# One table with an order of its own for each engine, from the last attention head to the MLP's second piece

## The chip, the cores and the metric

The kernel runs on one core of a Trainium2 chip. The metric is the time of one execution on the device in microseconds. Before the change it is 1332.62 us, the median of three runs (1331.37 to 1333.58). TensorE, VectorE (DVE), ScalarE (ACT), GpSimd (POOL) and SyncE (SP) each run a program of their own, in order, and wait for each other by semaphores.

## What is computed

Two layers over x of 2 x 1024 x 512 (batch, tokens, width), each followed by a layer norm of x plus the layer's result. Layer 1 is attention with 16 heads of 128 in which a token sees its own block of 64 and two on either side. Layer 2 picks the 128 tokens of each batch with the highest router score, and runs causal attention over the 256 of them (16 query heads, 8 key and value heads, rotary positions) and a gated MLP of 2048; all other tokens pass.

```
x = layernorm(x + (softmax(q k^T * scale + band) v) @ Wo)      # q, k, v = x @ Wq, Wk, Wv
idx = sort(top_k(x @ w_router, 128)); s = x[idx]; h = rms_norm(s) * ln1_w
q, k, v = rope(h @ wq + bq), rope(h @ wk + bk), h @ wv + bv
x1 = s + (softmax(causal(q k^T / sqrt(128))) v) @ wo
p = x1 + (silu(h2 @ w_gate) * (h2 @ w_up)) @ w_down             # h2 = rms_norm(x1) * ln2_w
x = layernorm(x + x.at[idx].set(g * p + (1 - g) * s))           # g = sigmoid(router score)
```

## The kernel before

A planner in Python writes the list `order`: one entry per job, such as ("scores", 31, 4). `job` (L327) appends an entry and numbers the semaphore steps that the engines will make for it (`SIGNALS`). `hold` notes who had a buffer last, so that `freed` can tell whom the next user waits for. Then each of five programs (tensor L916, scalar, vector, gpsimd, sync) walks through the same list and does its own part of each job, if it has one. So all engines take the jobs in one common order.

The planner runs over u, a tile of 128 queries of a head: at each u it puts down the scores of tile u, the transposes of tile u-1, the weighing of values of u-3, a half of a projection of the next head, an output projection tile, and whatever running generators (`tick`, `FLOW`) offer. The jobs of the stretch in question are these:

- Layer 1, head 31, the last: `scores` (TensorE into bank s0 or s1; DVE mask and maximum L1414; ACT exponential L1218), `norm` (DVE reciprocal and product, L1423), `tp` (TensorE transposes L989; ACT first half and DVE second half of a split into two fp32r numbers, L1180, L1379), `pv` (TensorE), `ot` (ACT and DVE split of a piece of the head's output), `out` (TensorE output projection of a token tile into bank y; DVE adds it, L1466). `qkfirst` and `qk` are the two halves of a projection.
- End of layer 1 for a token tile: `ln` (DVE statistics L1480, POOL reciprocal root L1663 on), `lnorm` (ACT; SP stores the tile), `lnscore` (DVE product with the router's weights, L1490).
- Choosing tokens: `rows` (TensorE, L1040, and ACT put the scores along a row), `count` and `tie` (DVE comparisons, L1506, L1511), `rank`, `prefixmm`, `prefix`, `findmm`, `find` (to the index of each chosen token), `gather` (POOL, two indirect DMAs, L1718 and L1723), `rin` and `rinx` (DVE, ACT, POOL: gate and norm), `rinh` (TensorE transposes L1071, ACT copy).
- Layer 2 attention of batch b: `p2half` and `p2` (TensorE, the two halves of piece n of the q, k, v projections, and the bias matmul L1088, which needs `ubias`), `p2r` (DVE, rotation, L1577 to L1582), `p2t` (TensorE transposes into bank y, L1097, ACT copy L1184), `p2v` (ACT copy), then for each of 8 key heads `as2` (scores; DVE maximum L1595, ACT exponential L1317), `an2` (DVE reciprocal L1604, ACT product L1328), `at2` (TensorE L1119, ACT), `av2` (TensorE, ACT), `o2` (TensorE). After them `res` and `resh`.
- MLP: `gu` (gate and up of 128 columns), `down`. `wsplit.n.G` or `.V` is the split of a 512 KB weight piece: ACT first half, POOL (L1690, 2.4 us) or DVE second half. `wload` is its DMA.
- `hload.n` (SP, L1811): the 512 KB DMA of the nth piece of layer 2's attention weights into one of 8 places (homes). SP waits for the job that read the place last (`emptied_by`), and only then issues, in the order of the list: hload.8 to .11 wait for p2half.0.0, p2.0.0, p2half.0.1, p2.0.1, hload.19 (weights of o2.0.3) for o2.0.0, hload.24 (first half of p2.1.0) for o2.0.2, hload.43 (of o2.1.3) for o2.1.0.

In names, the number after the kind is the head or the batch, then comes the tile or piece: tp.31.4, p2.0.7, as2.1.3.

Of the kernel before, what the change touches and what calls it, by code (L numbers as in the profile page):

```python
# [152 lines left out]
def build(nc, x, Wq, Wk, Wv, Wo, w_router, wq, wk, wv, wo, w_gate, w_up, w_down, ln1_w, ln2_w, bqkv, rope, out):  # L153
    with ExitStack() as ctx:
# [603 lines left out]
        for u in range(END + 4):  # L758
            H, i = divmod(u, TT)
            r, G = u % (HG * TT), u // (HG * TT)  # L760
# [117 lines left out]
        def weights(*key):  # L880

# [38 lines left out]
        def tensor_program(e):  # L920
            pe = Lane(e)
            pe.wait_ge(*G_.at("const", "ident"))
            for kind, *key in order:
                if kind == "turn":
                    b, t = key
                    dst = bank[bank_of["turn", b, t]]
# [30 lines left out]
                elif kind == "v":  # L957
                    G, t = key
# [11 lines left out]
                elif kind == "scores":  # L970
                    H, i = key
                    js = key_tiles(i)
                    n = len(js) * P
# [18 lines left out]
                elif kind == "pv":  # L992
# [22 lines left out]
                elif kind == "out":  # L1015
                    G, t = key
# [57 lines left out]
                elif kind in ("p2half", "p2"):  # L1074
                    b, n = key
# [16 lines left out]
                elif kind == "p2t":  # L1092
                    b, n = key
# [6 lines left out]
                elif kind == "as2":  # L1100
                    b, n = key
# [10 lines left out]
                elif kind == "at2":  # L1112
                    b, n = key
# [61 lines left out]
        def scalar_program(e):  # L1175
# [7 lines left out]

                e.activation(dst, src, ACT.Copy).then_inc(*S_.inc(*name, "copy"))  # L1184

            for kind, *key in order:
                if kind == "turn":
                    b, t = key
                    if b > 0:
# [17 lines left out]
                elif kind == "v":  # L1207
                    G, t = key
# [5 lines left out]
                elif kind == "scores":  # L1214
                    H, i = key
                    s, n = i % 2, len(key_tiles(i)) * P
# [5 lines left out]
                elif kind == "tp":  # L1222
                    H, i = key
                    js = key_tiles(i)
                    n = len(js)
# [26 lines left out]
                elif kind == "wsplit":  # L1252
                    n, _ = key
# [41 lines left out]
                elif kind == "p2v":  # L1295
                    b, n = key
# [5 lines left out]
                elif kind == "p2t":  # L1302
                    b, n = key
# [7 lines left out]
                elif kind == "as2":  # L1311
                    b, n = key
# [8 lines left out]
                elif kind == "an2":  # L1321
                    b, n = key
# [8 lines left out]
                elif kind == "at2":  # L1331
                    b, n = key
# [35 lines left out]
        def vector_program(e):  # L1368
# [17 lines left out]
            e.memset(counts[:], 0.0)  # L1386
            after(e.memset(ones_bf[:], 1.0), "const", "small")

            for kind, *key in order:
                if kind == "turn":  # L1390
                    b, t = key
                    cols = slice(t * P, (t + 1) * P)
# [9 lines left out]
                elif kind == "v":  # L1402
                    G, t = key
                    lo_part(vv[1][:, t, :], bank["proj1"][:, 0:GW], vv[0][:, t, :], "v", G, t)

                elif kind == "scores":
                    H, i = key
                    s, n = i % 2, len(key_tiles(i)) * P
# [8 lines left out]
                elif kind == "norm":  # L1417
                    H, i = key
                    s, n = i % 2, len(key_tiles(i)) * P
# [6 lines left out]
                elif kind == "tp":  # L1426
                    H, i = key
                    js = key_tiles(i)
                    n = len(js)
# [28 lines left out]
                elif kind == "out":  # L1458
                    G, t = key
# [9 lines left out]
                elif kind == "wsplit" and key[1] == "V":  # L1469
                    n = key[0]  # L1470
# [384 lines left out]
```

## Time and profile before

| | before |
|---|---|
| median of three runs | 1332.62 us |
| the profiled execution | 1332.4 us |
| its span, first to last instruction | 1330.3 us |
| TensorE busy | 1279.7 us (96%) |
| DVE, ACT, POOL busy | 781.6, 602.9, 243.3 us |
| mean granted TensorE clock | 0.986 |

The span starts at 0 with the first instruction. Head 31 begins at about 1048.5 us, layer 2's first projection at 1084.6, batch 1's first projection at 1170 and the MLP at 1251. The profiled execution takes 2.1 us more than its span. Busy time of TensorE can hold time in which its clock is lower: the granted clock stands beside it. "A <- B" in the views means that an instruction of A started late because of B.

### The profile page before, as it was taken

Reading aid. Unit: us, or ns where it says so; the run is one execution under the profiler, and the core shown is the slowest. Engines: PE = TensorE matmul, PEld = TensorE weight load, DVE = VectorE, ACT = ScalarE, POOL = GpSimd, SP = SyncE. Lnnn points to the kernel's source line nnn. Section 1 sums busy time; section 2 is a strip of 40 time slices with the busy share of each in tenths; the row PEclk is TensorE's granted clock in tenths of the full one; section 3 lists DMA queues with packets and bytes.
Section 4 is the critical chain, followed back from the end, with each engine's and each line's share of the span. In section 5 each row is a group of like instructions: output and inputs, shape, how many; then the busy total and the mean of one; then the engine's idle time right before and its main releaser. Section 6 shows DMA issues by size and latency. Waiting matters only on the chain.

```text
span 1330.3 us, 18968 instructions
## 1 busy us (share of the span) xinstructions
PE 1279.7 (96%) x7296; PEld 1092.9 (82%) x7296; DVE 781.6 (59%) x2187; ACT 602.9 (45%) x1422; POOL 243.3 (18%) x218
## 2 busy tenths in 40 slices
PE   7999999999999999999999999999999978999897
PEld 6898989898989898978798989898989853545696
DVE  4656565656665656676667765656565667542243
ACT  4544445454444444545444444444444442433453
POOL 2101111111111110134120212111111142000064
PEclk9999999999999999999999999999999988999899
DMA  5000111110001202032310101010101055565064
GB/s 183 31 33 32 33 32 32 33 32 33 33 32 33 80 1 79 1 103 90 109 49 17 48 28 46 28 48 17 48 17 48 27 180 162 184 208 162 0 198 135
DMA packets 62410, 89.33 MB, mean 67 GB/s; under 512 B 3232, under 2 KB 36000, under 8 KB 62320
## 3 DMA queue, kind: packets, MB, share of 16 engines
q1 hardware_dynamic: 61904, 86.81, 20.0%
q0 software_dynamic: 416, 1.31, 0.3%
q8 instruction: 57, 0.93, 0.3%
q14 instruction: 33, 0.27, 0.1%
HBM read 79.20 MB, written 8.91 MB: 66 GB/s over the span
## 4 chain that ended last, share of the span: by engine, by line
PE 87%; DVE 7%; ACT 4%; issue 1%; POOL 1%; DMA 1%; SPq 0%; POOLq 0%
PE proj L909 41%; PE y L909 13%; PE s L909 10%; PE o L909 9%; PE tp L989 5%; PE proj L917 3%; PE s L917 3%; DVE arena L1379 2%; ACT arena L1180 2%; PE o L917 1%; ACT prob L1218 1%; DVE prob L1414 1%; DVE products L1490 1%; DVE prob L1423 1%; DVE yacc L1466 1%
## 5 line engine op out<-in xcount | busy, mean ns | idle before, releaser
L909 PE MATMUL proj<-arena 128*128 128x256 f32 (+1 forms) x3408 | 625.5, 332 | 7.2 <-DVE arena L1379 6.3
L909 PEld LDWEIGHTS proj<-arena 128*128 128x128 f32 x3408 | 521.8, 190 | 65.4 <-DVE arena L1379 8.2
L1218 ACT ACTIVATE prob<-prob,stat 128x384 f32<-128x384 f32 (+1 forms) x256 | 151.0, 590 | 443.5 <-DVE stat L1414 443.5
L1690 POOL TENSOR_TENSOR arena<-wraw,arena 128x1024 fp32r<-128x1024 f32 x75 | 182.2, 2439 | 832.3 <-ACT arena L1180 814.0
L1379 DVE TENSOR_TENSOR arena<-proj,arena 128x512 fp32r<-128x512 f32 (+1 forms) x256 | 142.7, 558 | 274.2 <-ACT arena L1180 272.4
L909 PE MATMUL y<-arena 128*128 128x512 f32 x810 | 211.0, 396 | 0.3 <-DVE yacc L1466 0.3
L1379 DVE TENSOR_TENSOR arena<-tp,arena 128x384 fp32r<-128x384 f32 (+2 forms) x258 | 134.9, 523 | 108.4 <-ACT arena L1180 108.2
L909 PE MATMUL o<-arena 128*128 128x256 f32 (+2 forms) x960 | 196.2, 324 | 0.5 <-DVE arena L1379 0.5
L909 PE MATMUL s<-arena 128*128 128x384 f32 (+2 forms) x870 | 191.5, 333 | 3.0 <-DVE arena L1379 3.0
L1180 ACT ACTIVATE arena<-proj 128x512 fp32r<-128x512 f32 (+1 forms) x256 | 124.3, 486 | 118.5 <-PE proj L909 115.5
L909 PEld LDWEIGHTS s<-arena 128*128 128x128 f32 x870 | 151.8, 189 | 20.3 <-DVE arena L1379 4.5
L909 PEld LDWEIGHTS y<-arena 128*128 128x128 f32 x810 | 147.4, 189 | 24.7 <-DVE yacc L1466 0.7
L909 PEld LDWEIGHTS o<-arena 128*128 128x128 f32 x960 | 136.8, 190 | 1.7 <-DVE arena L1379 1.2
L1414 DVE CUSTOM_DVE_ANT_0 prob<-s,band 128x384 f32<-128x384 f32 (+1 forms) x256 | 131.9, 515 | 0.0
L989 PE MATMUL tp<-ident,prob 128*128 128x128 f32 x704 | 119.9, 274 | 7.1 <-DVE prob L1423 7.1
L1180 ACT ACTIVATE arena<-tp 128x384 fp32r<-128x384 f32 (+2 forms) x258 | 117.9, 457 | 10.5 <-PE tp L989 7.9
L1423 DVE TENSOR_SCALAR prob<-prob,stat 128x384 f32<-128x384 f32 (+1 forms) x256 | 113.8, 445 | 9.1
L989 PEld LDWEIGHTS tp<-ident,prob 128*128 128x128 f32 x704 | 85.9, 140 | 24.7 <-DVE prob L1423 13.9
L1466 DVE TENSOR_TENSOR yacc<-y,yacc 128x512 f32<-128x512 f32 x127 | 87.1, 686 | 17.1 <-PE y L909 17.0
L1180 ACT ACTIVATE arena<-wraw 128x1024 fp32r<-128x1024 f32 x88 | 90.3, 1055 | 2.3 <-DMA wraw<-in_L_ffn_w_up 1.8
L917 PE MATMUL proj<-late 128*128 128x512 f32 x120 | 58.6, 612 | 0.0
L1180 ACT ACTIVATE arena<-o 128x512 fp32r<-128x512 f32 (+1 forms) x74 | 42.0, 568 | 22.6 <-PE o L1071 14.7
(156 smaller groups left out, 686.0 us busy)
## 6 DMA issues: line engine op xcount, KB each, us to landing
wraw<-in_L_attn_Wq SPq DMA_DIRECT2D x16, 512.0 KB, 3.4
wraw<-in_L_attn_Wk SPq DMA_DIRECT2D x16, 512.0 KB, 3.3
wraw<-in_L_attn_Wv SPq DMA_DIRECT2D x16, 512.0 KB, 3.4
wraw<-in_L_attn_Wo SPq DMA_DIRECT2D x16, 512.0 KB, 3.7
late<-in_L_ffn_wq SPq DMA_DIRECT2D x16, 512.0 KB, 4.7
late<-in_L_ffn_wo SPq DMA_DIRECT2D x16, 512.0 KB, 3.9
yacc<-in_L_attn_hidden_states SPq DMA_DIRECT2D x16, 256.0 KB, 3.0
y_dram<-yacc SPq DMA_DIRECT2D x16, 256.0 KB, 3.0
```

The lines of the kernel that those rows point to most:

```text
L909: ins = e.matmul(out_ap, l[a], r[b], start=first and i == 0 and j == 0, stop=final and i == n - 1 and j == 2, skip_group_check=skip)
L917: ins = e.matmul(out_ap, l, r, start=first and i == 0, stop=final and i == n - 1, skip_group_check=skip)
L989: ins = e.transpose(bank["tp"][:, m * P:(m + 1) * P], prob[i % 2][:, m * P:(m + 1) * P], ident[:])
L1180: e.activation(dst, src, ACT.Copy).then_inc(*S_.inc(*name, "hi"))
L1218: e.activation(prob[s][:, 0:n], prob[s][:, 0:n], ACT.Exp, bias=stat[:, 4 * s + 1:4 * s + 2], scale=-1.0, accum_out=stat[:, 4 * s + 2:4 * s ...
L1379: e.tensor_tensor(dst_lo, src, dst_hi.bitcast(F32), ALU.subtract).then_inc(*V_.inc(*name, "lo"))
L1414: e.tensor_tensor_reduce(prob[s][:, 0:n], bank[f"s{s}"][:, 0:n], reach, -SCALE, -NEG, ALU.add, ALU.min, nm).then_inc(*V_.inc("scores", H, ...
L1423: e.tensor_scalar(prob[s][:, 0:n], prob[s][:, 0:n], rc, None, ALU.mult).then_inc(*V_.inc("norm", H, i, "prob"))
L1466: e.tensor_tensor(yacc[:, t, :], bank[bank_of["out", G, t]][:, :], yacc[:, t, :], ALU.add).then_inc(*V_.inc("out", G, t, "sum"))
L1490: e.tensor_tensor_reduce(products[:], row, router[:], 1.0, 0.0, ALU.mult, ALU.add, score[:, c:c + 1]).then_inc(*V_.inc("lnscore", b, t, "s ...
L1690: e.tensor_tensor(lo, wraw[n % RAW_SLOTS][:], hi.bitcast(F32), ALU.subtract).then_inc(*G_.inc("wsplit", n, "lo"))
```

## The change

`job` no longer numbers steps; it only notes what the job holds. A new function `comes(n, engines)` gives job n to some engines: it appends it to their programs, numbers their steps, and settles at the first call who frees the buffers. All jobs before scores.31.0 are given to all engines, in the old order. Then the table `LAST` is read: each word is an engine (T, S, V, G) and a job. Whatever it doesn't name comes afterwards in the old order. No word of the table names D, the program of SP, so SP's list is the old one. It names 164 jobs of TensorE, 158 of DVE, 134 of ACT and 19 of POOL, from scores.31.0 to gu.1 and the weight splits behind it. The instructions of a job are not touched.

The buffers' succession stays the same but for bank y: p2t.0.0 now has it between out.15.5 and out.15.6, and before it came after out.15.6.

How far jobs move in an engine's list, the larger moves:

- TensorE: scores.31.1 to 31.7 come 3 to 6 jobs earlier, rinh.0 7 later; p2t.0.0 4 earlier, out.15.6 and 15.7 3 later; p2.0.4 to p2.0.7 2 to 11 earlier, with av2.0.0 9 later, o2.0.0 11, o2.0.1 10, o2.0.2 8, o2.0.3 9; rinh.1 4 later, after o2.0.6. In batch 1 p2.1.4 to p2.1.7 are 1 to 9 earlier, o2.1.0 15 later, o2.1.1 14.
- DVE: rin.0 13 and rinx.0 11 earlier, ubias 18 later, p2r.0.0 13 earlier, p2r.0.4, p2r.0.5 11 earlier; ln.1.7 12 later, lnscore.1.7 14 later, the split of weight piece 68 19 later.
- ACT: rinh.0 7 later, lnorm.1.7 4 later, splits 66 and 67 19 and 47 later, split 68 19 earlier.
- POOL: split 65 behind ln.1.2, 66 behind ln.1.3, 67 behind gather.1.

```diff
+LAST_HEAD = ("scores", 31, 0)
+LAST = """
+S.scores.31.0 S.tp.30.7 S.rin.0 S.qk.31.k.1 S.scores.31.1 S.tp.31.0 S.scores.31.2 S.o.30.1 S.tp.31.1 S.scores.31.3
+S.qk.31.q.1 S.tp.31.2 S.tp.31.3 S.scores.31.4 T.scores.31.0 T.qkfirst.31.k.1 T.scores.31.1 T.tp.30.7 T.qk.31.k.1
+T.scores.31.2 T.out.14.4 T.tp.31.0 T.pv.30.5 T.pv.30.6 T.scores.31.3 T.out.14.5 T.pv.30.7 T.tp.31.1 T.qkfirst.31.q.1
+T.qk.31.q.1 T.tp.31.2 T.out.14.6 T.scores.31.4 T.tp.31.3 T.scores.31.5 T.pv.31.0 T.out.14.7 T.pv.31.1 T.tp.31.4
+T.scores.31.6 T.pv.31.2 T.out.15.0 T.tp.31.5 T.scores.31.7 T.rinh.0 T.pv.31.3 T.out.15.1 T.pv.31.4 T.tp.31.6
...
+V.out.15.2 V.ln.1.2 V.lnscore.1.0 V.ot.4 V.tp.31.7 V.out.15.3 V.lnscore.1.1 V.ubias V.ot.5 V.lnscore.1.2 V.ln.1.3
+V.count.1.0.0 V.out.15.4 V.count.1.1.before V.p2r.0.0 V.ot.6 S.wsplit.65.G S.scores.31.5 S.ot.0 S.tp.31.4 S.ot.1
...
+S.tp.31.7 S.ot.5 S.lnorm.1.2 S.rows.1.0 S.ot.6 G.rin.0 G.ln.1.0 G.ln.1.1 T.out.15.2 T.p2half.0.0 T.tp.31.7 T.pv.31.5
+T.out.15.3 T.pv.31.6 T.p2.0.0 T.rows.1.0 T.out.15.4 T.pv.31.7 T.p2half.0.1 T.out.15.5 T.p2.0.1 T.p2t.0.0
+T.p2half.0.2 T.rows.1.1 T.out.15.6 T.out.15.7 T.p2t.0.1 T.p2.0.2 T.p2half.0.3 S.lnorm.1.3 S.wsplit.66.G S.p2t.0.0
...
+T.as2.0.0 T.p2.0.3 T.as2.0.1 T.rows.1.2 T.p2half.0.4 T.p2.0.4 T.p2half.0.5 T.p2t.0.3 T.p2.0.5 T.at2.0.0 T.as2.0.2
+T.p2half.0.6 T.at2.0.1 T.p2t.0.4 T.rows.1.3 T.p2.0.6 T.as2.0.3 T.av2.0.0 T.p2half.0.7 T.p2t.0.5 T.p2.0.7 T.at2.0.2
+T.as2.0.4 T.av2.0.1 T.o2.0.0 T.at2.0.3 T.as2.0.5 T.av2.0.2 T.o2.0.1 T.av2.0.3 T.p2t.0.7 T.prefixmm.1 T.at2.0.4
+T.o2.0.2 T.findmm.1 T.as2.0.6 T.av2.0.4 T.at2.0.5 T.o2.0.3 T.as2.0.7 T.at2.0.6 T.av2.0.5 T.o2.0.4 T.av2.0.6
+T.at2.0.7 T.o2.0.5 T.av2.0.7 T.o2.0.6 T.rinh.1 T.o2.0.7 T.p2half.1.0 T.p2.1.0 T.p2half.1.1 T.p2.1.1 V.count.1.4.3
...
+G.ln.1.2 G.wsplit.65.G G.ln.1.3 G.wsplit.66.G G.ln.1.4 G.ln.1.5 G.ln.1.6 G.ln.1.7 G.gather.1 G.wsplit.67.G G.rin.1
...
+"""
...
         def job(kind, *key):
             order.append((kind,) + key)
-            if kind == "wsplit":
...
+            taken.append(taking[:])
+            taking.clear()
...
+        program = {eng: [] for eng in "TVSGD"}
+
+        def comes(n, engines):
+
+            kind, *key = order[n]
+            for space, who, steps, name in taken[n]:
+                room[who, space] = holder.get(space)
+                holder[space] = (steps, name)
+            taken[n] = []
+            signals = SIGNALS["wsplit" + key[1] if kind == "wsplit" else kind] if kind in SIGNALS or kind == "wsplit" else {}
+            for eng in engines:
+                program[eng].append(order[n])
+                for name in signals.get(eng, ()):
+                    ENGINES[eng].plan(kind, *(key[:1] if kind == "wsplit" else key), name)
...
+        turning = number_of[LAST_HEAD]
+        for n in range(turning):
+            comes(n, "TVSGD")
+        placed = set()
+        for line in LAST.split():
+            eng, kind, *key = line.split(".")
+            n = number_of[(kind,) + tuple(int(k) if k.isdigit() else k for k in key)]
+            comes(n, eng)
+            placed.add((eng, n))
+        for n in range(turning, len(order)):
+            comes(n, [eng for eng in "TVSGD" if (eng, n) not in placed])
...
-            for kind, *key in order:
+            for kind, *key in program["T"]:
```

The other four programs read `program["S"]`, `["V"]`, `["G"]` and `["D"]` likewise.

## Rows read from the trace of the kernel before

**Rows 1.** The page: span, and TensorE and its granted clock in 40 slices

```profile
span 1330.3 us, 18968 instructions
...
PE   7999999999999999999999999999999978999897
...
PEclk9999999999999999999999999999999988999899
```

**Rows 2.** Windows: from:to length, busy us (instructions) PE PEld DVE ACT POOL, clock, DMA

```profile
1048.50:1060.80 12.30, 12.30 (x65) 10.53 (x64) 7.61 (x21) 4.19 (x11) 0.00 (x0) 1.00 0.01 2
1060.80:1104.00 43.20, 35.90 (x149) 25.14 (x148) 30.06 (x85) 17.12 (x38) 21.03 (x41) 0.92 0.53 178
1104.00:1122.50 18.50, 13.68 (x32) 5.90 (x30) 12.59 (x46) 4.84 (x12) 5.00 (x12) 0.72 0.44 148
1122.50:1157.70 35.20, 31.67 (x122) 16.32 (x122) 22.29 (x96) 12.96 (x45) 0.00 (x0) 1.00 0.62 194
1157.70:1170.00 12.30, 11.45 (x42) 7.42 (x42) 4.59 (x19) 7.73 (x24) 2.80 (x4) 0.87 0.43 148
1170.00:1246.00 76.00, 70.26 (x233) 37.48 (x232) 23.45 (x73) 28.36 (x74) 0.74 (x2) 1.00 0.45 145
1246.00:1252.00 6.00, 1.46 (x8) 1.25 (x9) 3.54 (x7) 1.88 (x2) 0.74 (x2) 0.80 0.00 0
```

**Rows 3.** Windows, same columns: the stretches with a lower granted clock

```profile
1068.00:1076.00 8.00, 6.60 (x24) 5.25 (x23) 4.95 (x15) 5.27 (x12) 3.78 (x2) 0.57 0.88 331
...
1109.00:1120.00 11.00, 9.31 (x17) 4.09 (x17) 6.25 (x25) 2.49 (x4) 2.16 (x5) 0.53 0.25 85
...
1156.00:1162.00 6.00, 4.51 (x15) 3.48 (x16) 2.11 (x10) 3.25 (x11) 2.05 (x2) 0.72 0.42 137
```

**Rows 4.** Timeline of TensorE: start, us, instruction, [idle before <-who ended it]

```profile
1067.30 0.55 PE L989 MATMUL tp<-ident,prob 128*128 128x128 f32 x3 [1.91 <-DVE prob L1423]
...
1108.45 0.63 PE L1097 MATMUL y<-ident,late 128*128 128x128 f32 x4 [3.14 <-DVE late L1582]
...
1157.49 1.12 PE L1097 MATMUL y<-ident,late 128*128 128x128 f32 x4 [1.93 <-DVE late L1582]
```

**Rows 5.** Waits of TensorE, 1048 to 1252: us in total, times, longest

```profile
PE y L1097 <- DVE late L1582: 8.9, 6, 3.1
PE tp L989 <- DVE prob L1423: 4.8, 4, 1.9
...
PE o L1040 <- DVE score L1490: 1.6, 1, 1.6
```

**Rows 6.** Timelines of DVE and of POOL, in the last head

```profile
1074.76 2.38 DVE L1423 TENSOR_SCALAR prob<-prob,stat 128x384 f32<-128x384 f32 x1
...
1072.22 4.70 POOL L1690 TENSOR_TENSOR arena<-wraw,arena 128x1024 fp32r<-128x1024 f32 x2 [6.19 <-ACT arena L1180]
```

**Rows 7.** The page's costliest groups: line, engine, shapes | busy us, mean ns

```profile
L1218 ACT ACTIVATE prob<-prob,stat 128x384 f32<-128x384 f32 (+1 forms) x256 | 151.0, 590 | 443.5 <-DVE stat L1414 443.5
...
L1414 DVE CUSTOM_DVE_ANT_0 prob<-s,band 128x384 f32<-128x384 f32 (+1 forms) x256 | 131.9, 515 | 0.0
...
L1423 DVE TENSOR_SCALAR prob<-prob,stat 128x384 f32<-128x384 f32 (+1 forms) x256 | 113.8, 445 | 9.1
```

**Rows 8.** The router products' line: duration ns min/median/max, first and last start

```profile
L1490 DVE CUSTOM_DVE_ANT_0 products<-yacc,router x16: 680/683/2344, 576.4 to 1112.6; 128x512 bf16<-128x512 f32 x16
```

**Rows 9.** DMA issues, 1110 to 1222: KB each, median us to landing

```profile
late<-in_L_ffn_wq SPq DMA_DIRECT2D x10, 512.0 KB, 4.5
```

**Rows 10.** The chain that ended last: start, us, what

```profile
1159.32 2.96 DMA late<-rope,position
...
1170.19 1.72 PE proj L917 x4
1171.91 1.72 PE s L917 x4
```

**Rows 11.** Waits of DVE, 1048 to 1252: us in total, times, longest

```profile
DVE arena L1379 <- ACT arena L1180: 15.6, 12, 2.4
...
DVE stat L1604 <- ACT prob L1317: 6.9, 6, 1.2
DVE yacc L1466 <- PE y L909: 6.2, 5, 4.0
```

More of the change, by code:

```diff
@@ new lines @@
+T.p2half.0.2 T.rows.1.1 T.out.15.6 T.out.15.7 T.p2t.0.1 T.p2.0.2 T.p2half.0.3 S.lnorm.1.3 S.wsplit.66.G S.p2t.0.0
+S.rows.1.1 S.lnorm.1.4 V.lnscore.1.3 V.out.15.5 V.ln.1.4 V.count.1.1.0 V.tie.1.0 V.ln.1.5 V.p2r.0.1 V.out.15.6
+V.tie.1.1 V.ln.1.6 V.count.1.0.1 V.out.15.7 V.count.1.1.1 V.lnscore.1.4 V.lnscore.1.5 V.lnscore.1.6
+V.count.1.2.before V.count.1.2.1 V.as2.0.0 V.count.1.3.before V.count.1.3.1 V.tie.1.2 V.ln.1.7 V.p2r.0.3 V.as2.0.1
+V.tie.1.3 V.an2.0.0 V.count.1.0.2 V.count.1.1.2 V.p2r.0.4 V.count.1.2.2 V.lnscore.1.7 V.count.1.3.2 V.an2.0.1
@@ new lines @@
+V.count.1.4.before V.p2r.0.5 V.as2.0.2 V.count.1.4.2 V.count.1.5.before V.count.1.5.2 V.tie.1.4 V.tie.1.5
+V.count.1.0.3 V.an2.0.2 V.as2.0.3 V.count.1.1.3 V.count.1.2.3 V.count.1.3.3 S.p2t.0.1 S.lnorm.1.5 S.lnorm.1.6
+S.as2.0.0 S.rows.1.2 S.p2v.0.2 S.lnorm.1.7 S.an2.0.0 S.p2t.0.3 S.as2.0.1 S.at2.0.0 S.an2.0.1 S.as2.0.2 S.p2t.0.4
+S.rows.1.3 S.as2.0.3 S.at2.0.1 S.an2.0.2 S.av2.0.0 S.p2t.0.5 S.an2.0.3 S.at2.0.2 S.av2.0.1 S.as2.0.4 S.at2.0.3
+S.wsplit.67.G S.av2.0.2 S.wsplit.68.V S.an2.0.4 S.p2v.0.6 S.as2.0.5 S.at2.0.4 S.p2t.0.7 S.av2.0.3 S.an2.0.5
@@ new lines @@
+V.count.1.5.3 V.an2.0.3 V.count.1.6.before V.count.1.6.3 V.count.1.7.before V.as2.0.4 V.p2r.0.7 V.count.1.7.3
+V.an2.0.4 V.tie.1.6 V.tie.1.7 V.rank.1 V.as2.0.5 V.prefix.1 V.an2.0.5 V.find.1 V.as2.0.6 V.an2.0.6 V.as2.0.7
+V.an2.0.7 V.rin.1 V.rinx.1 S.av2.0.4 S.as2.0.6 S.at2.0.5 S.an2.0.6 S.at2.0.6 S.as2.0.7 S.av2.0.5 S.an2.0.7 S.av2.0.6
+S.at2.0.7 S.av2.0.7 S.rinh.1 S.rin.1 S.resh.0 S.p2t.1.0 S.p2v.1.2 S.p2t.1.1 S.p2t.1.3 S.as2.1.0 S.an2.1.0 S.as2.1.1
+S.at2.1.0 S.as2.1.2 S.an2.1.1 S.at2.1.1 S.an2.1.2 S.as2.1.3 S.p2t.1.4 S.an2.1.3 S.av2.1.0 S.p2t.1.5 S.at2.1.2
@@ new lines @@
+G.ln.1.2 G.wsplit.65.G G.ln.1.3 G.wsplit.66.G G.ln.1.4 G.ln.1.5 G.ln.1.6 G.ln.1.7 G.gather.1 G.wsplit.67.G G.rin.1
+G.res.0 G.res.1 T.p2t.1.0 T.p2half.1.2 T.p2.1.2 T.p2half.1.3 T.resh.0 T.p2.1.3 T.p2t.1.1 S.av2.1.1 S.at2.1.3
+S.as2.1.4 S.av2.1.2 S.p2t.1.7 S.an2.1.4 S.as2.1.5 S.av2.1.3 S.an2.1.5 S.at2.1.4 S.as2.1.6 S.p2v.1.6 S.at2.1.5
+S.an2.1.6 S.av2.1.4 S.as2.1.7 S.av2.1.5 S.at2.1.6 S.an2.1.7 V.p2r.1.0 V.p2r.1.1 V.res.0 V.resh.0 V.p2r.1.3 V.as2.1.0
+V.an2.1.0 V.as2.1.1 V.an2.1.1 V.p2r.1.4 V.as2.1.2 V.p2r.1.5 V.as2.1.3 V.an2.1.2 V.an2.1.3 V.p2r.1.7 V.as2.1.4
@@ L127, in compares @@
+T.gu.1 G.gu.0 G.gu.1 G.wsplit.70.G S.resh.1 V.res.1 V.resh.1 V.gu.0 V.gu.1 V.wsplit.69.V S.gu.0 S.gu.1 S.wsplit.69.V
+S.wsplit.70.G
+"""
 def compares():
@@ L329, in build @@
         ENGINES = dict(T=T_, V=V_, S=S_, G=G_)
-        order = []
+        order, taken, taking = [], [], []
         holder, room = {}, {}
@@ L1184, in whole_copy @@
                 e.activation(dst, src, ACT.Copy).then_inc(*S_.inc(*name, "copy"))
-            for kind, *key in order:
+            for kind, *key in program["S"]:
                 if kind == "turn":
@@ L1387, in vector_program @@
             after(e.memset(ones_bf[:], 1.0), "const", "small")
-            for kind, *key in order:
+            for kind, *key in program["V"]:
                 if kind == "turn":
@@ L1683, in gpsimd_program @@
             pool.wait_ge(*V_.at("const", "small"))
-            for kind, *key in order:
+            for kind, *key in program["G"]:
                 if kind == "wsplit" and key[1] == "G":
@@ L1758, in sync_program @@
             sp = Lane(e)
-            for kind, *key in order:
+            for kind, *key in program["D"]:
                 if kind == "router":
```

21 lines of the change are left out of this document (12 added, 9 removed).

## The prediction

> **What bounds the kernel now.** I first read the page's 40 slices [rows 1]. The reader should see TensorE at nine tenths nearly everywhere and its granted clock below full in the last fifth. The span is 1330.3 us. Next I cut the changed stretch into windows [rows 2]: from 1048.5 us, where the last head's scores begin, to 1246, where batch 1's output projection ends. TensorE idles 5.7 + 1.6 us in the last head and the end of layer 1 (7.3 in the window 1060.8 to 1104, 5.7 of it before 1084.6), 18.50 - 13.68 = 4.8 at the layer change, 3.5 during batch 0's attention, 0.85 to 1170 and 5.7 in batch 1. That is 22.2 us. Another 4.5 us lie behind 1246.
>
> The granted clock is a second loss [rows 3]. While it was 0.57, 6.60 us were busy, which is 6.60 x 0.43 = 2.8 us lost. The other two are 9.31 x 0.47 = 4.4 and 4.51 x 0.28 = 1.3, together 8.5. A piece of idle time lies in front of each, or at its start: 1.91 us ending at 1067.30, 3.14 ending at 1108.45 and 1.93 ending at 1157.49 [rows 4]. The first two windows are nearly all at the lower level (1.2 GHz), the third for about half its time, and from 1122.5 to 1157.7 the grant is 1.00 (2.4 GHz) [rows 2, 3]. So 22.2 + 8.5 = 30.7 us is all that an order can give here: the matmuls stay the same.
>
> Third, the waits [rows 5]. 8.9 us of them are a transpose of a rotated q or k that waits for DVE's sum, 4.8 are probability transposes waiting for DVE's normalisation, and 1.6 the scores' rows waiting for a router product. All are waits for one job of an engine that is itself not full: DVE is busy 7.6 + 30.1 + 12.6 + 22.3 = 72.6 of the 109.2 us up to the index of the chosen tokens [rows 2]. TensorE's own work up to there is 12.3 + 35.9 + 13.7 + 31.7 = 93.6 less 7.2 of clock, that is 86.4. TensorE is therefore the bound if both are fed, with DVE second.
>
> **The change, part by part.** No instruction is added or dropped; the jobs' numbers follow each engine's new list. SP ("D") is in no line of the table and keeps the old order.
>
> *Last head.* TensorE now issues scores.31.1 and scores.31.2 ahead of transposes 30.7 and 31.0, so that a tile's chain (mask and maximum, exponential, normalisation, transpose, two splits) runs a tile ahead. The 1.91 us [rows 4] are such a transpose waiting. Stepping through the new list with the durations of the timelines, each transpose's probabilities are there 0.4 to 1.7 us before TensorE comes to it, and the splits of the last head's output (ot) 0.1 to 1.3 us. The idle 5.7 and the 2.8 of clock go, and I leave 1.0: +7.5 (bounds 8.5 and 1.7, if three waits of the size of 1.91 and half the clock remain). DVE's routing work of batch 0 (rin.0, rinx.0) comes earlier in it, beside out.14 jobs that keep TensorE busy.
>
> *POOL.* The weight splits 65 and 66 move behind ln.1.2 and ln.1.3, and 67 behind the gather. Now splits 66 and 67 hold POOL for 4.70 us, and DVE's normalisation beside them takes 2.38 us [rows 6] where its mean is 0.45 [rows 7]. One blocked DVE instruction costs 1.93, and that one goes (it is in the 7.5). In their new place the splits run beside router products, the bias split (ubias) and a rope sum. The router product has been blocked too: 2.344 us against a median of 0.683 [rows 8]. ubias stands right in front of the bias matmul of p2.0.0. I put one block of 1.7 on TensorE's path there, and 0.8 for pv.31.6, which follows transpose 31.7 with less between than before. The rows.1.0 wait of 1.6 [rows 5] goes, as it now comes after p2.0.0 and pv.31.6. This piece is 1.6 - 2.5 = -0.9; its bounds are +1.6 (no block) and 1.6 - 5.1 - 0.8 = -4.3 (three blocks).
>
> The page SBUF — State Buffer of the Trainium skill, section Who interferes with whom, states this as a rule: a DVE instruction with two SBUF inputs, or one in a 2-port mode, and a GpSimd instruction that reads SBUF exclude each other for a whole instruction. The two long rows agree. By that rule alone, any of the splits that meets such a DVE instruction would add up to 2.4 us to DVE; without it this part would be a gain of 1.6.
>
> *Layer change.* p2t.0.0 moves ahead of out.15.6 and out.15.7, p2r.0.0 ahead of ot.6 and the ties on DVE. Before, DVE came to p2r.0.0 only behind lnscore.1.4, ln.1.6 and ln.1.7, and TensorE waited 3.14 us for it [rows 4]. Now ln.1.7 comes 12 places later. Of 4.8 idle and 4.4 clock I leave 1.0: +8.2 (bounds 9.2 and 3, with two waits of 1 to 2 us and the clock low again). What is late next is lnscore.1.7, 14 places later: rows.1.3 needs it, and it is some 2.6 us ahead of TensorE in my stepping. On SP the store of that tile (lnorm.1.7) stands before hload.13, and behind it queue loads 14 to 18. I have it issued some 8 us before p2.0.6 needs it; a load lands in 4.5 us [rows 9], so 3 us are to spare.
>
> *Batch 0.* TensorE does all projections (p2.0.3 to p2.0.7) first and puts off av2 and o2: o2.0.0 by 11 places. This fills the wait for the softmax with 1.72 us pieces [rows 10] and brings p2r.0.7 out of the token chain's way. New waits: all as2.0.x share bank s0, and as2.0.5 waits for DVE's maximum of as2.0.4, behind two long counts (about 0.9); prefixmm waits for rank (0.9). Behind findmm stand 4 attention quarters with four o2 of 1.72, about 10.2 us, over the chain find, gather (its second DMA 2.96 [rows 10]), rin, rstd, rinx of about 8.7: 1.5 to spare, and I allow 1.5 of idle, since DVE may still be at an2.0.7. Loss before: 3.5 + 0.85 + 1.3 = 5.7. I leave 3.5 (0.9, 0.9, 1.5 and 0.2): +2.2. Bounds: +5.7 and -6.
>
> *SP's unchanged order.* hload.19 waits for o2.0.0, and loads 20 to 23, needed by o2.0.4 to o2.0.7, stand behind it; 24 and 25 (batch 1's first piece) wait for o2.0.2. From o2.0.0 to o2.0.3, which reads load 19, TensorE has 7.3 us of other work against the 4.5 of a load. Batch 1 is alike: load 43 opens at o2.1.0, and 7.8 us lie before o2.1.3. I cost it at nothing; the cover is 2.8 us, and if gone a load costs up to 4.5. wload.68 has to wait for split 65, which ends around 1083 in the new order, before hload.11: nothing.
>
> *Batch 1.* The same shift (o2.1.0 by 15 places) takes the rope waits out: 5.7, of which I leave 1.5: +4.2 (bounds 5.7 and 1.5). The end (res.1, resh.1, 4.5 us idle [rows 2] and the clock of 0.80 there) has the same chain and stays.
>
> Sum: 7.5 - 0.9 + 8.2 + 2.2 + 4.2 = 21.2. Span 1330.3 - 21.2 = 1309.1. The profiled execution took 1332.4, 2.1 more than its span: 1311.2. The median of the runs, 1332.62, is 0.2 above it: **1311.5 us**. Differences of under about 0.2% (2.7 us) cannot be told from no change here.
>
> **Rivals.**
> (a) *DVE becomes the bound.* For: it has waited 15.6 us for ScalarE's first halves and 6.2 for TensorE's out [rows 11], and an in-order engine keeps such waits if the neighbours shift with it. If they and the 6.9 for exponentials stay, DVE needs 72.6 + 28.7 = 101.3, plus 3.7 for blocks less 1.93, about 103 of the 109.2 us: 6 us gained there, 4.2 in batch 1, 1332.6 - 10.3 = 1322. Against: ot, tp and out now have a job of another kind between them nearly everywhere. 12%.
> (b) *Nearly everything closes.* All 30.7 would give 1302; with a fourth of my 9.5 left over, 1304. 10%.
> (c) *Slower: the weights.* Place: SP's queue, loads 19 to 33 and 43 to 47, now opened by postponed o2 jobs. If a load is opened only one piece before it is needed, a piece of 1.72 us [rows 10] hides less than half of its 4.5 us and TensorE waits 2.8 each time. Fifteen such waits are 42 us: 1332.6 - 21.2 + 42 = 1353. It decides for slower from 9 such waits on (23.9 / 2.8). Against: the 7.3 us counted above; none of the waits named above is for a landing. 5%.
> (d) *The order changes nothing*, since the two prob buffers set the pace and not the lists. Against: maximum 0.52, exponential 0.59, normalisation 0.45 [rows 7] and transposes 0.55 [rows 4] are 2.1 us for a buffer, one tile in 1.1 us with two, and between 1060.8 and 1104 TensorE has (35.9 - 2.8) / 5 = 6.6 us of work for each of the five tiles left [rows 2, 3]. Within 0.2%: 3%.
>
> **How the numbers follow.** Forecast 70% (own range 1304 to 1320, with the 9.5 of residues between a fourth and nearly twice), (a) 12%, (b) 10%, (c) 5%, (d) 3%. The range must leave out no more than 2 in 10: 1303.5 takes in half of (b), 1321 a part of (a). Faster: 70 + 12 + 10 = 92, less 1 for the part of (a) that runs out near nothing, 91%; same 3%; slower 6%.
>
> **What would show it.** Right: no idle over 1 us before the probability transposes of head 31; p2half.0.0 starting 8 to 9 us earlier than 1084.6; clock 1.00 through the layer change; DVE busy above 80% up to the index; batch 1's first piece near 1144 to 1150 instead of 1170; the distance from there to the MLP 4 us shorter. Wrong: a TensorE wait that a weight's DMA ends (c); findmm later than 1148 (a); a router product, ubias or rope sum of 2.3 us more than once; rinh.1 with idle of over 2 us before it.

## The result, and the profile after

The changed kernel takes 1300.29 us (median of 4 runs, 1299.84 to 1302.11) and the kernel before, run beside it, 1333.1 (ratio 0.9753, 95% interval 0.9731 to 0.9775). My forecast was 1311.5, with a range from 1303.5 to 1321. The direction was right, and the gain of 33 us is half as large again as the 21.2 I had summed, outside the range.

The page of the changed kernel (the profiled execution took 1302.1 us), in the same rows as [rows 1]: span, then busy time and the clock granted to TensorE in 40 slices.

```profile
span 1300.3 us, 18971 instructions
PE 1267.5 (97%) x7296; PEld 1089.4 (84%) x7296; DVE 783.2 (60%) x2187; ACT 600.4 (46%) x1422; POOL 243.8 (19%) x218
...
PE   7999999999999999999999999999999999999897
...
PEclk9999999999999999999999999999999999999899
```

The dent in TensorE's row and the two slices of its clock at eight tenths beside it are gone; the one at the MLP's start is left. The instructions are as before: the same work, in other turns.

Next the waits of TensorE from 1048 to 1222 us in the changed kernel (us in total, times, longest), which answer to [rows 5], and their places in its timeline (idle time in brackets), which answer to [rows 4]:

```profile
PE o L1145 <- DVE works L1695: 3.3, 1, 3.3
PE proj L1162 <- DVE arena L1529: 2.1, 1, 2.1
PE o L1145 <- DVE works L1632: 1.1, 1, 1.1
PE y L1171 <- DVE yacc L1540: 0.5, 1, 0.5
```

```profile
1076.24 1.88 PE L991 MATMUL proj<-late 128*128 128x512 f32 x4
...
1084.57 0.49 PE L1162 MATMUL proj<-arena,unit_row 40*128 40x512 f32 x1 [2.07 <-DVE arena L1529]
...
1094.44 0.66 PE L1171 MATMUL y<-ident,late 128*128 128x128 f32 x4 [0.46 <-DVE yacc L1540]
...
1147.42 0.66 PE L1145 MATMUL o<-ident,works 128*128 128x128 f32 x4 [1.15 <-DVE works L1632]
...
1219.57 1.09 PE L1145 MATMUL o<-ident,works 128*128 128x128 f32 x4 [3.31 <-DVE works L1695]
```

Twenty-six idle pieces of over 0.1 us have become five: those of the four rows with brackets, and 1.41 us right behind the last of them. No probability transpose waits any more, and no transpose of a rotated q or k waits for its rotation: from 1147.4 to 1216, all of batch 1, there is no idle time. The first row is layer 2's first projection, 8.3 us earlier than in the kernel before. Three waits are left ahead of the MLP. The bias matmul of p2.0.0 waits for `ubias`, which is two instructions of DVE, the unit row (L1525) and the lower half of the split behind it (L1529): 2.07. The transposes p2t.0.0 wait for bank y, which the residual sum of out.15.5 has to free: 0.46. And rinh.1 waits for the end of the token chain: 1.15.

In the windows the changed stretch, up to the MLP's first matmul, reads as follows, first in the kernel before and then in the one after (from:to, length, busy us and instructions of PE, PEld, DVE, ACT and POOL, granted clock, DMA's share, GB/s):

```profile
1048.75:1251.17 202.42, 175.63 (x639) 102.95 (x637) 103.09 (x342) 76.57 (x203) 30.31 (x61) 0.95 0.46 149
```

```profile
1050.30:1222.07 171.77, 163.38 (x637) 99.63 (x636) 105.24 (x342) 74.32 (x203) 31.71 (x61) 0.98 0.51 175
```

The stretch is 30.65 us shorter. Idle time gives 26.79 - 8.39 = 18.4 of it. The other 12.25 are *busy* time, for the same matmuls. The clock accounts for part: before, 8.5 were lost [rows 3]; after, there is one fall ahead of 1216, in the window of 8 us behind the 2.07 us wait, and it costs 7.43 x 0.21 = 1.6:

```profile
1084.00:1092.00 8.00, 7.43 (x23) 5.25 (x24) 6.49 (x17) 2.42 (x4) 3.31 (x7) 0.79 0.31 106
```

So 12.25 - 6.9 = 5.3 us of busy time are neither recorded idle time nor clock. My sum had no term for them.

### The profile page after: what moved, and what is told of

Same layout as the page of the kernel before. It is cut to its first block, busy times and chain, and to the rows that moved or that the text cites. A ratio compares the mean times of both kernels' runs of the same rounds, so it can differ in the third digit from the quotient of the medians.

```text
span 1300.3 us, 18971 instructions
## 1 busy us (share of the span) xinstructions
PE 1267.5 (97%) x7296; PEld 1089.4 (84%) x7296; DVE 783.2 (60%) x2187; ACT 600.4 (46%) x1422; POOL 243.8 (19%) x218
## 4 chain that ended last, share of the span: by engine, by line
PE 89%; DVE 5%; ACT 3%; DMA 1%; issue 1%; POOL 1%; SPq 0%; POOLq 0%; ACTq 0%
PE proj L983 42%; PE y L983 13%; PE s L983 10%; PE o L983 9%; PE tp L1063 5%; PE proj L991 4%; PE s L991 2%; DVE arena L1453 2%; ACT arena L1254 1%; PE o L991 1%; ACT prob L1292 1%; DVE products L1564 1%; DVE prob L1488 1%; DVE yacc L1540 1%; DMA wraw<-in_L_attn_Wq 0%
## 5 line engine op out<-in xcount | busy, mean ns | idle before, releaser
L1254 ACT ACTIVATE arena<-tp 128x384 fp32r<-128x384 f32 (+2 forms) x258 | 118.0, 457 | 12.9 <-PE tp L1063 10.3
```

The source lines that it names most:

```text
L1254: e.activation(dst, src, ACT.Copy).then_inc(*S_.inc(*name, "hi"))
```

## The experiments

Two theories on the missed 11 us were set against each other first. Theory H: every wait of TensorE costs some 0.2 us more than its recorded idle time. Theory P: the sum was right in kind, and the surplus lies in batch 1. Three kernels build the change up piece by piece, and a fourth run repeats the whole.

In the diffs below a line is a run of words of one engine's list around the edit, not a line of the file; the words that follow are left out at the marks.

**l1_head.** The table's new order ends with the last head (TensorE's words are shown); the jobs behind it have the old order. The weight splits are an exception here and in the next two kernels: they keep the table's new places on POOL and ScalarE.

```diff
 T.tp.31.7 T.pv.31.5 T.out.15.3
-T.pv.31.6 T.p2.0.0 T.rows.1.0 T.out.15.4 T.pv.31.7 T.p2half.0.1
+T.rows.1.0 T.p2.0.0 T.pv.31.6 T.out.15.4 T.p2half.0.1 T.pv.31.7
...
```

> The table's own orders only for the jobs up to tp.31.7 (the last head); every later job in the old common order. Nothing is left out of the computation. Theory H (every wait of TensorE hides some 0.2 us more than its recorded idle time, because the end of the matmul before it is modelled later than the next one could start): the head's recorded loss of 5.7 idle and 2.8 clock plus 8 waits x 0.2 go, 1333.1 - 9.5 = about 1323.5. Theory P (the prediction's sum was right in kind, the surplus is batch 1's): 1333.1 - 7.5 = 1325.5.

Measured 1322.34 us (1321.95 to 1325.57), against 1332.3 of the kernel before on the same chip: -10.0, where my term for the head was 7.5 (and a part of POOL's -0.9, which comes with the splits, is in it too). The early head meets a layer change in the old order, and a wait for a rope sum stands there that is larger than any of the kernel before. TensorE's timeline of this kernel:

```profile
1080.55 0.43 PE L1113 MATMUL o<-ident,score 128*128 128x128 f32 x2 [1.59 <-DVE score L1563]
...
1101.13 1.09 PE L1170 MATMUL y<-ident,late 128*128 128x128 f32 x4 [4.57 <-DVE late L1655]
1103.42 1.11 PE L1170 MATMUL y<-ident,late 128*128 128x128 f32 x4 [1.20 <-ACT late L1257]
```

**l2_change.** The new order ends at layer 2's fifth projection half (p2half.0.4).

```diff
 T.rows.1.2 T.p2half.0.4
-T.p2.0.4 T.p2half.0.5 T.p2t.0.3 T.p2.0.5
+T.at2.0.0 T.p2t.0.3 T.p2.0.4 T.av2.0.0
...
```

> The table's own orders up to p2half.0.4 (last head and layer change), the old common order from there on. Theory H: the head's 9.5, then 1.6 + 9.2 of recorded loss and 3 waits x 0.2, less the 2.1 us wait for ubias and the clock behind it (1.6): 1333.1 - 17.5 = about 1315.5. Theory P: 1333.1 - 14.8 = 1318. The trace shows in both the wait of the bias matmul L1162 of about 2.1 us.

Measured 1319.04 (1316.87 to 1320.75): -3.3 more, where the terms of POOL and of the layer change were 7.3 together. The 4.57 us are gone, but behind the new order batch 0's old one waits 1.9 us for a rope sum, 2.6 for probabilities and 2.5 for copies of ScalarE (L1257), and the bias matmul's wait is now 2.1 (0.78 in l1_head).

**l3_batch0.** The new order ends ahead of batch 1, which has the old one.

```diff
 T.rinh.1
-T.o2.0.7 T.p2half.1.0 T.p2.1.0
+T.p2half.1.0 T.o2.0.7 T.p2.1.0
...
```

> The table's own orders up to the end of batch 0 (before p2half.1.0), batch 1 in the old common order. Theory H: batch 1 keeps its recorded 5.4 to 5.7 us of idle time and 7 waits x 0.2, so this is 7.1 slower than the changed kernel: 1307.5. Theory P: the surplus of 11 us over the prediction lies in batch 1, so this is 4.2 + 11 = 15 slower than the changed kernel: 1315.

Measured 1311.44 (1310.7 to 1315.14): -7.6 more, where the term was 2.2.

**after_again.** The changed kernel without an edit, on the same chip.

> The changed kernel on the same chip as its three parts: 1300.3 in both theories, 0.9753 of the kernel before; it fixes the distance to the three others.

Measured 1300.79 (1300.34 to 1302.27): -10.65 more, where the term was 4.2. The increments 10.0, 3.3, 7.6 and 10.65 sum to 31.5 against 21.2. By these times neither theory holds throughout: measured were 1322.3, 1319.0 and 1311.4, where H had 1323.5, 1315.5 and 1307.5 and P had 1325.5, 1318 and 1315. Neither had an entry for the waits that a part moved alone hands on to the next.

More than half of the difference of 10.3 comes with batch 1, the simplest of the parts. From the start of its first projection piece to the start of its last output piece, less a piece of batch 0 of 1.72 us where one stands inside, the traces have 72.1 us before, 73.2 in l3_batch0 and 64.8 after. That is 7.4 to 8.4, where the recorded idle time that went is only 5.6 to 6.2, in 7 and 8 waits, and the granted clock is 1.00 in all three. So a part without any routing work and without a fall of the clock gives about 2 us more than its idle time. (The step of 10.65 is larger than 8.4 because l3_batch0's profile has the fall behind the 2.07 us wait, 1.7 us, and after_again's has not, and a wait of 0.69 stood in front of batch 1.)

To see what, I split the same stretch of every kernel, from the end of scores.31.0 to the end of the first gate/up piece: its length, TensorE's recorded idle time, the number of waits of over 0.1 us, busy time lost to a lower clock (busy time times one less the granted clock), and the rest.

| kernel | stretch | idle | waits | clock | rest |
|---|---|---|---|---|---|
| before | 207.8 | 26.8 | 26 | 11.8 | 169.2 |
| l1_head | 197.4 | 23.0 | 19 | 6.4 | 168.0 |
| l2_change | 194.5 | 20.6 | 18 | 6.2 | 167.8 |
| l3_batch0 | 185.8 | 15.4 | 14 | 3.9 | 166.4 |
| after | 176.2 | 8.4 | 5 | 3.8 | 164.0 |
| after_again | 174.7 | 8.3 | 5 | 2.2 | 164.2 |
| both (below) | 173.1 | 6.4 | 3 | 2.7 | 164.0 |
| both_outfirst (below) | 171.4 | 4.8 | 2 | 2.7 | 164.0 |

The rest is the same matmuls at full clock in all rows. It falls with the number of waits, from 26 to 5 by 5.0 to 5.2 us, 0.24 for each, and is 164.0 to 164.2 with five or fewer; the four profiles that the table leaves out (control, ubias_early, pool_late, sp_follows, 4 or 5 waits) have 163.7 to 164.1. The number of falls of the clock goes down as well, but it isn't the reason: "after" has one more than after_again and no larger rest.

The reason can be read from rows. Here are two output projection pieces of the kernel before, four matmuls each of one shape, the first behind a wait and the second in a full queue:

```profile
1167.81 1.95 PE L917 MATMUL s<-late 128*128 128x512 f32 x4 [0.40 <-ACT late L1184]
...
1171.75 1.88 PE L917 MATMUL s<-late 128*128 128x512 f32 x4
```

In the full queue the four are shown as 1.88 us, but the next matmul starts 1.71 us after their start. The end of a matmul is modelled, and where TensorE waits idle time is counted only from that modelled end, 0.16 us late. And the first matmul behind a wait takes longer: it is shown with 0.67 us instead of 0.59 (128x512), a transpose with 0.30 to 0.33 instead of 0.27. Over the 20 waits of the kernel before that lie outside the falls of the clock, the two together are 0.22 us on average, which is read from single instructions and not from the table. In the trace the weight load of such a matmul starts only 0.03 us ahead of it; that this makes it longer I only argue.

The next kernels ask what the waits that are left come from. Theory A: the job stands too late in its engine's list. Theory B: POOL's weight split holds up DVE. The rows that led to the question are these, of DVE and then of POOL in the changed kernel:

```profile
1081.51 2.29 DVE L1525 TENSOR_TENSOR unit_row<-ident 40x8 fp32r<-40x8 f32 x1
...
1091.25 2.52 DVE L1564 CUSTOM_DVE_ANT_0 products<-yacc,router 128x512 bf16<-128x512 f32 x1
```

```profile
1081.37 2.41 POOL L1764 TENSOR_TENSOR arena<-wraw,arena 128x1024 fp32r<-128x1024 f32 x1
...
1090.80 2.42 POOL L1764 TENSOR_TENSOR arena<-wraw,arena 128x1024 fp32r<-128x1024 f32 x1 [1.97 <-ACT arena L1254]
```

**ubias_early.** DVE's list alone is edited.

```diff
-V.ot.2 V.out.15.1
+V.ot.2 V.ubias V.out.15.1
...
-V.lnscore.1.1 V.ubias V.ot.5
+V.lnscore.1.1 V.ot.5
```

> The changed kernel with one word moved: DVE splits the bias rows (ubias) right behind ot.2, before POOL's weight split 65 can start. Theory B (POOL's split, which begins 0.14 us before, blocks DVE's two-input instruction and with it the bias matmul of p2.0.0): the wait of 2.07 us before L1162 goes, with 0.24 hidden behind it and in some executions 1.6 of clock; DVE is 0.9 later for the last head, which costs at most 0.5: 1300.5 - 2.3 to - 3.9, about 1297.5. Rival (the bias matmul would wait anyway, for p2.0.0's turn in DVE's or ScalarE's list): within 0.5 of the changed kernel.

Measured 1299.0 (1298.69 to 1300.03), 1.4 under the unchanged copy (control, below), where 2.3 to 3.9 under it were expected. The unit row takes 0.15 us, the 2.07 us wait is gone, and no clock fall follows. But the splits now hold up two router products (one in the changed kernel), and TensorE's wait in front of p2t.0.0 grows to 1.66. DVE's rows and TensorE's row of this kernel:

```profile
1081.73 2.54 DVE L1563 CUSTOM_DVE_ANT_0 products<-yacc,router 128x512 bf16<-128x512 f32 x1
...
1088.58 2.59 DVE L1563 CUSTOM_DVE_ANT_0 products<-yacc,router 128x512 bf16<-128x512 f32 x1
```

```profile
1091.84 0.66 PE L1170 MATMUL y<-ident,late 128*128 128x128 f32 x4 [1.66 <-DVE yacc L1539]
```

**pool_late.** DVE's list as in the changed kernel, POOL's edited.

```diff
-G.ln.1.2 G.wsplit.65.G G.ln.1.3 G.wsplit.66.G
+G.ln.1.2 G.ln.1.3 G.wsplit.65.G G.wsplit.66.G
```

> Only POOL's order differs from the changed kernel: its split of weight 65 stands behind its part of the LayerNorm of tile 3 of layer 1, instead of in front of it; VectorE's unit row stays where the change put it. Theory B (the small two-input instruction of VectorE is slow because POOL's 128x1024 subtraction reads at the same time): the row of unit_row is 0.15 us instead of 2.29, and TensorE's wait of 2.07 us before the bias matmul shrinks by about 2 us, to under 0.5; the split now meets another two-input instruction of VectorE, so time comes out 0 to 2 us under the changed kernel's 1300.4. Theory A (the job stands too late in VectorE's own turns, POOL has nothing to do with it): the row stays above 2 us or the wait stays near 2.07 us.

Measured 1303.08 (1299.17 to 1304.64): the time is 2.7 over the unchanged copy, where 0 to 2 under it were expected; the mechanism is as theory B has it. With ubias where the change put it, its instruction takes 0.15 us and the 2.07 us wait is gone. The two splits now run back to back, 5.14 us from 1087.36 on, and hold up two other instructions that read two operands from SBUF. DVE's rows:

```profile
1082.21 0.15 DVE L1524 TENSOR_TENSOR unit_row<-ident 40x8 fp32r<-40x8 f32 x1
...
1087.67 2.62 DVE L1655 TENSOR_TENSOR late<-late 128x512 f32<-128x512 f32 x1
...
1090.55 2.50 DVE L1563 CUSTOM_DVE_ANT_0 products<-yacc,router 128x512 bf16<-128x512 f32 x1
```

and TensorE's wait with the window behind it, where the granted clock is 0.50, the lower level (1.2 GHz), for 6.8 us:

```profile
1093.72 1.12 PE L1170 MATMUL y<-ident,late 128*128 128x128 f32 x4 [2.73 <-DVE yacc L1539]
```

```profile
1092.80:1099.60 6.80, 5.88 (x13) 3.52 (x14) 4.87 (x15) 1.49 (x3) 4.21 (x12) 0.50 0.00 0
```

One block of 2.1 us has become 1.9 + 1.8, and 5.88 x 0.50 = 2.9 us of clock came with it. The splits are as long as before; what they meet on DVE has changed. Not all of the 2.7 us is the edit's: this profile has another fall of 6.8 us from 10.7 us on, far ahead of the edit, with 6.07 us busy in it, 3.0 us lost.

**sp_follows.** Words for SP: loads that need not wait for o2.0.0 go ahead of load 19, which does, and the same in batch 1.

```diff
+D.hload.18 D.hload.20 D.hload.22 D.hload.23 D.hload.25 D.hload.27 D.hload.19 D.hload.21 D.hload.24
...
+D.hload.30 D.hload.32 D.hload.31 D.hload.33
...
+D.hload.42 D.hload.44 D.hload.46 D.hload.47 D.hload.43 D.hload.45
```

> The changed kernel with a list for SP too: the weight loads 19 to 30 and 39 to 47 in the order in which their places come free in TensorE's new list (20, 22, 23, 25, 27 ahead of 19, and so on), the rest as it was. Theory Q (SP's old order holds the free places back until o2.0.0 and then lets nine loads go at once, which stretches the rope gather from 3.0 to 6.4 us and makes rinh.1 wait 0.7 to 1.15): that wait goes, and the DMA share between 1114 and 1130 us rises from 0.06 to over 0.4: 1300.5 - 1.2 = 1299.3. Rival (the gather is late for its own reasons): the gather stays above 5 us and the time within 0.4 of the changed kernel.

Measured 1300.54 (1299.24 to 1301.22): no difference from the unchanged copy that can be told. The trace did change. In the changed kernel SP stood from 1113.5 at load 19 until o2.0.0 was made, and then issued nine loads of 512 KB within 9.4 us (1130.0 to 1139.4), beside the gather that the token chain waits for. Its chain there:

```profile
1136.56 1.10 POOL x_sel L1792
1137.66 0.30 issue
1137.96 6.35 DMA late<-rope,position
1144.31 0.02 issue
1144.33 0.69 DVE products L1621
```

The second gather took 6.35 us, where it took 2.96 before [rows 10]. The windows 1114 to 1130 and 1136 to 1145 show the burst, in the changed kernel and then in sp_follows:

```profile
1114.00:1130.00 16.00, 16.00 (x61) 8.48 (x60) 13.80 (x59) 8.56 (x31) 0.00 (x0) 1.00 0.42 155
...
1136.00:1145.00 9.00, 9.00 (x37) 5.54 (x37) 2.25 (x15) 5.57 (x20) 4.42 (x3) 1.00 0.98 357
```

```profile
1114.00:1130.00 16.00, 16.00 (x65) 8.90 (x64) 13.79 (x58) 8.36 (x32) 0.00 (x0) 1.00 0.87 309
...
1136.00:1145.00 9.00, 9.00 (x33) 5.14 (x32) 3.41 (x15) 5.32 (x19) 5.12 (x5) 1.00 0.74 226
```

With DMA at 0.74 instead of 0.98, the second gather takes 3.50 us, DVE has the gathered rows 5.4 us after the index, not 8.3, and TensorE's wait before rinh.1 (1.15) is gone from the trace. All profiles agree: 5.9 to 6.4 us for this gather in the five kernels with the whole table and SP's old order, 3.2 to 3.5 in the three with SP's new one. (The expectation's 0.06 is the DMA share of 1120 to 1130; from 1114 to 1130 it is 0.42.) Worth at most 1.15 + 0.24 us, it does not show in the medians.

**both.** The edits of ubias_early and sp_follows together.

> Both edits together, the moved ubias and SP's own list. If they are independent, 1300.5 - 2.9 - 1.2 = 1296.4, with idle time left only at the MLP's start (3.3 + 1.4) and 0.5 to 0.8 us before the first rope transpose. If the time saved ahead only brings TensorE sooner to a token chain that isn't ready, rinh.1 waits again and it is no better than the better of the two (1297.5).

Measured 1298.48 (1297.43 to 1299.03), 1.9 under the unchanged copy: short of the 1296.4, since the moved ubias alone had already brought 1.4 and not 2.9. rinh.1 doesn't wait, so the other case isn't what happened either. Ahead of the MLP only the wait of 1.66 is left.

**control.** The changed kernel, unchanged, beside these three.

> The changed kernel once more as the measure for the three others: 1300.5, 0.9755 of the kernel before, in both theories. Its profile shows whether the clock falls behind the 2.07 us wait (1302 in the profiled execution) or not (1300.3).

Measured 1300.37 (1299.86 to 1302.43). Its profiled execution, the one of 1302.43, has the fall behind the wait (2.06).

**both_outfirst.** In both, DVE does the residual sum that TensorE waits for, and one LayerNorm's moments, ahead of the router product that the split would hold up.

```diff
-V.lnscore.1.3 V.out.15.5 V.ln.1.4 V.count.1.1.0
+V.out.15.5 V.ln.1.4 V.lnscore.1.3 V.count.1.1.0
```

> The version with both edits (1298.5 us), and in it VectorE adds the last y piece of group 15's tile 5 and takes the moments of tile 4 ahead of the router product of tile 3, which POOL's split holds up for 2.6 us. If the 1.66 us wait of TensorE that is left in the layer change comes only from that place in the queue, it goes, and the time is 1.7 + 0.24 = 1.9 us lower, 1296.6 (1296.0 to 1297.5). If the split then holds up the next job just as long, the wait only moves on and the time stays at 1298.5 within 0.5.

Measured 1297.29 (1296.05 to 1297.67), ratio 0.9725 (0.9707 to 0.9743), against 0.9746 (0.9729 to 0.9763) of both: the fastest here, some 3 us under the changed kernel, and 0.7 above the 1296.6 expected, inside the range given with it. The intervals overlap; what is sure is the trace, in which the 1.66 is gone and TensorE has no wait at all between the last head and the MLP. The split and the DVE instructions beside it:

```profile
1088.98 2.36 POOL L1769 TENSOR_TENSOR arena<-wraw,arena 128x1024 fp32r<-128x1024 f32 x1 [0.60 <-ACT arena L1259]
```

```profile
1089.30 0.68 DVE L1545 TENSOR_TENSOR yacc<-y,yacc 128x512 f32<-128x512 f32 x1
1089.89 0.68 DVE L1559 BATCH_NORM_STATS2 bn_out<-yacc 128x6 f32<-128x512 f32 x1
1090.61 0.18 DVE L1560 BATCH_NORM_AGGREGATE mv<-bn_out 128x2 f32<-128x6 f32 x1
1090.71 1.18 DVE L1569 CUSTOM_DVE_ANT_0 products<-yacc,router 128x512 bf16<-128x512 f32 x1
```

A sum with one operand in PSUM and the moments of one SBUF operand run at their usual 0.68 beside the split; the router product, with two SBUF operands, takes 1.18 and ends only after the split's end at 1091.34.

A sharper measure than the medians lies in the traces. In the twelve profiles TensorE's matmul 101 starts anywhere from 28.8 to 31.1 us, with the same lists, and from there to the end of scores.31.0 all of them take 1019.7 to 1020.0 us. So the stretch from the end of scores.31.0 to the MLP's first matmul compares the tables without the spread of the start. It is 171.7 in the changed kernel and 171.4 in control (both with a fall behind the 2.07 us wait), 170.1 in after_again (without it), 172.2 in pool_late, 170.5 in sp_follows (with it), 168.7 in ubias_early, 167.7 in both and 166.0 in both_outfirst. SP's list is then worth 0.9 to 1.1 us beside the kernels with the fall and 1.0 between ubias_early and both; the last edit is worth 1.7, and pool_late is 0.6 to 0.9 slower than the two with the fall. These are single executions.

## Why the prediction was wrong

**The cap.** The step that failed is "22.2 + 8.5 = 30.7 us is all that an order can give here: the matmuls stay the same". It took the recorded idle time and the clock for the whole loss and put everything else at nothing. A wait also costs 0.24 us of time that the record shows as busy; with 21 waits gone that is 5.0 to 5.2 us. The clock had more to give as well. The three falls are 6.8, 10.2 and 3.4 us at 0.50 with 5.62, 9.17 and 3.40 us busy in them, which is 9.1 and not 8.5. Behind 1246 the kernel before has a fall of 6.8 us with 5.42 us busy, the changed one too, but it starts earlier against the 3.3 us wait and has 4.23 busy: 0.6. With all this the cap would have been 37 to 38, and the gain of 32 to 33 inside it. With the waits' 5.2 alone the forecast would have been 1306.3 and the range's lower end 1298.3 (1303.5 - 5.2): this term is what put the result outside.

**The residues.** I left 9.5 us. The changed kernel's trace has 2.07 + 0.46 + 1.15 = 3.7 us of idle time up to 1216 and 1.6 of clock, together 5.3; after_again's has no fall there, and 3.6 in all. So the residues were too large by 4.2. Between the two profiled executions the stretch of the table above is 31.6 us shorter, 10.4 more than my 21.2: 4.2 of residues, 5.2 of waits and 1.0 of clock. In the medians the miss is 11.2; the other 0.8 is not accounted for.

**Point by point.**
- Last head: right. No transpose of head 31 waits (0 left against my 1.0); the forecast of p2half.0.0 8 to 9 us earlier came out at 8.3.
- POOL and ubias: right in place and mechanism. I put "one block of 1.7 on TensorE's path there"; the row is 2.29 where it takes 0.15 unblocked, and TensorE's wait 2.07. The 0.8 for pv.31.6 did not come. The sign "a router product, ubias or rope sum of 2.3 us more than once" did come (2.29 and 2.52), and it wasn't a sign of a slower kernel: of the two only the first is waited for at length. The Trainium skill, page SBUF — State Buffer, section Who interferes with whom, says that a DVE instruction with two SBUF inputs contends with a GpSimd instruction that reads SBUF, and one with at most one SBUF input, outside the 2-port modes, does not. The runs agree on both: 2.29 us for a sum of 40x8 elements, and 0.68, as ever, for the residual sum with one input in PSUM (both_outfirst).
- Layer change: mechanism right, except "clock 1.00 through the layer change". Six profiles have the bias matmul's wait at 2.06 to 2.09 us; in four of them (after, control, sp_follows, l3_batch0) a fall of 3.4 us follows it within 0.7 us, in two (after_again, l2_change) it doesn't. What decides stays open.
- Batch 0: mis-sized. I left 3.5 (rank, a maximum, the chain, the clock); 1.15 is there (0.73 in after_again), and findmm came at 1135.8, well ahead of the bound of 1148. The waits of 0.9 that I priced for as2.0.5 and prefixmm did not come.
- SP's unchanged order: "I cost it at nothing" was nearly right in its size and wrong in its reason. I looked for a TensorE wait for a weight, and there was none; the held-back loads hit the token gather (6.35 against 2.96). Of the 3.4 us at most 1.15 reached TensorE, within the 1.5 that I had allowed for the chain.
- Batch 1: mis-sized. I left 1.5 and nothing was left; the 4.2 became 7.4 to 8.4, with the cost of the waits. Its first piece starts at 1149.6, inside the 1144 to 1150 of the forecast, and from there to the MLP it is 7.0 us less, not 4.
- MLP's start: idle as forecast (3.31 + 1.41 before and after).

**The rivals.** (a) fell: DVE is busy 30.04 of 34.70 us in the last head and 73.98 of 85.70 up to the index, both above the 80% of my sign, but its waits for ScalarE's halves shrank from 15.6 [rows 11] to 7.2 us, and of the three waits that DVE still gives TensorE ahead of the MLP's start the only one over 1.2 us is the blocked one. (c) fell: no TensorE wait ends with a weight's DMA. (d) fell with the time itself. (b) was the nearest: nearly everything closed, and its 1304 was bounded by the same cap of 30.7. As the forecast it would still have been 3.7 us high.

**Additivity.** The parts don't price singly: alone, the head moved a wait of 4.57 us to the layer change, and the layer change alone left waits to batch 0. A term of the sum is worth what I wrote only with its neighbours in place.

## What to carry to other kernels

Count the waits of the bounding engine as well as their length: here each of 21 cost TensorE 0.24 us that its record showed as busy, so idle time plus clock is not the cap of what an order can give. When jobs of one engine's list are postponed, look at what its opened buffers release in a burst, and which small transfer on a dependent chain that burst meets. Beside a POOL instruction on large tiles put DVE jobs that read PSUM or one operand from SBUF, and first among them the job that another engine waits for. Where executions start with a spread of their own (2.3 us here), compare the changed stretch and not only the whole time.

## What the hardware showed that I had not expected

- A 40x8 addition of two SBUF operands took 2.29 us instead of 0.15 beside a POOL subtraction of 2.41: the block does not scale with the blocked instruction's size (a 128x512 router product took 2.52 us instead of 0.68 beside one of 2.42).
- A gather landed in 6.35 us instead of 2.96 with the DMA engines at 0.98 busy and 357 GB/s.
- The same wait of 2.06 to 2.09 us was followed by 3.4 us at half the clock in two executions of the same kernel and by none in a third; with a wait of 2.73 in pool_late went 6.8.
- The first matmul behind a wait was shown with 0.30 to 0.33 us instead of 0.27 (128x128) and 0.67 instead of 0.59 (128x512).
